# Attention scores from three bf16 parts, FFN tables built during the attention, and value products issued in pairs of sets

## The reference

```python
qkv = layernorm(x) @ Wqkv                       # x: 2 x 1024 x 512; 32 heads of 16, one shared k and v
scores = einsum("bqhd,bkd->bhqk", q, k) * 16**-0.5 + slope[h] * (pos_k - pos_q)   # causal
attn = einsum("bhqk,bkd->bqhd", softmax(scores), v) @ Wo
x = x + layernorm(attn)
W = (code4bit - (zero4bit + 1)) * scale         # Wg, Wu: 512 x 1376, Wd: 1376 x 512, groups of 128 rows
x = x + layernorm((silu(ln(x) @ Wg) * (ln(x) @ Wu)) @ Wd)
```

## Time and profile before

| | |
|---|---|
| median of three runs | 1397.24 us (1396.83 to 1401.67) |
| profiled execution, its own time | 1395.92 us |
| its span, first to last instruction | 1394.1 us |
| mean granted TensorE clock | 0.956 of 2.4 GHz |
| PE, DVE, ACT, POOL busy over the span | 89%, 52%, 41%, 22% |

### The profile page before, as it was taken

One profiled execution on the slowest core, in us unless ns is written; L12 is line 12 of the kernel. 1 busy time (PEld: TensorE's weight loads), 2 busy tenths in 40 slices (PEclk: granted clock), 3 DMA queues, 4 the chain that ended last, 5 costly groups with the idle time before them and its releaser, 6 DMA issues. The chain is left out here.

```text
span 1394.1 us, 16630 instructions
## 1 busy us (share of the span) xinstructions
PE 1239.7 (89%) x6208; PEld 826.8 (59%) x6208; DVE 730.3 (52%) x1353; ACT 571.8 (41%) x1006; POOL 308.0 (22%) x329
## 2 busy tenths in 40 slices
PE   4599999999999999989992389999999999579995
PEld 4567456555554656544541257778778788346664
DVE  4376785786688887723214666342141210365553
ACT  5143455265456565556661344311111111034443
POOL 0121141111110101011124344411121111115554
PEclk9999999899999999999996599999999999889998
DMA  6534223201221012122001422230020010130303
GB/s 194 112 54 113 43 40 106 40 2 39 47 56 25 23 19 40 25 40 40 18 31 51 124 72 62 94 106 0 0 91 1 0 61 1 59 105 1 121 0 120
DMA packets 60942, 75.97 MB, mean 54 GB/s; under 512 B 14738, under 2 KB 37530, under 8 KB 60796
## 3 DMA queue, kind: packets, MB, share of 16 engines
q1 hardware_dynamic: 57252, 64.42, 18.7%
q0 software_dynamic: 2560, 8.39, 1.7%
q10 hardware_dynamic: 1056, 2.16, 0.4%
HBM read 53.46 MB, written 21.59 MB: 54 GB/s over the span
## 5 line engine op out<-in xcount | busy, mean ns | idle before, releaser
L792 DVE TENSOR_REDUCE mx<-bank 128x1 f32<-128x512 f32 (+2 forms) x576 | 367.3, 685 | 138.7 <-PE bank L910 85.1
L734 ACT ACTIVATE PT<-ST 128x512 f32<-128x512 f32 x576 | 313.3, 600 | 210.3 <-PE ST L975 90.0
L907 PE MATMUL bank<-KS,QS 126*128 126x512 f32 (+2 forms) x896 | 253.3, 365 | 18.1 <-DMA QS<-pos_scratch 15.8
L975 PE MATMUL ST<-QS,KS 128*128 128x512 f32 x576 | 240.1, 457 | 5.0 <-DMA QS<-mparts 4.1
L907 PEld LDWEIGHTS bank<-KS,QS 126*128 126x128 f32 x896 | 158.7, 197 | 82.9 <-DVE mx L792 37.7
L975 PEld LDWEIGHTS ST<-QS,KS 128*128 128x128 f32 x576 | 108.3, 195 | 82.6 <-ACT PT L734 64.1
L989 PE MATMUL PO<-PT,V 128*32 128x512 f32 x1152 | 152.2, 604 | 1.6 <-ACT PT L734 1.6
L51 PE MATMUL f_pair<-f_xT,gu 128*128 128x512 f32 (+1 forms) x352 | 142.1, 404 | 0.0
L1495 DVE TENSOR_TENSOR f_h<-f_h,f_pair 128x512 f32<-128x512 f32 (+1 forms) x44 | 30.2, 686 | 210.1 <-ACT f_h L1402 210.1
L53 PE MATMUL f_pair<-f_xT,gu 128*128 128x512 f32 (+1 forms) x352 | 139.8, 397 | 0.0
L52 PE MATMUL f_pair<-f_xT,gu 128*128 128x512 f32 (+1 forms) x352 | 139.4, 396 | 0.0
(11 more groups left out here) (181 smaller groups left out, 1777.6 us busy)
## 6 DMA issues: line engine op xcount, KB each, us to landing
QS<-q_scratch SPq DMA_DIRECT2D x48, 256.0 KB
q_scratch<-QP SPq DMA_DIRECT2D x24, 256.0 KB, 2.3
l_x<-x_dram SPq DMA_DIRECT2D x12, 512.0 KB, 4.2
xres<-_attn_hidden_states_dram POOLq DMA_DIRECT2D x16, 256.0 KB, 3.0
x_dram<-xout POOLq DMA_DIRECT2D x16, 256.0 KB, 2.4
f_xin<-x_dram SPq DMA_DIRECT2D x4, 1024.0 KB, 7.0
f_xsum<-x_dram SPq DMA_DIRECT2D x4, 1024.0 KB, 6.9
x_dram<-f_xsum SPq DMA_DIRECT2D x4, 1024.0 KB, 4.8
```

The lines of the kernel that those rows point to most:

```text
L734: act.activation(PT[:, quad % PT_RING, n % 4, :], ST[:, n % ST_RING, :], ACT.Exp).then_inc(p_done, 1)
L792: v.tensor_reduce(mx[:, i % 2, z, h:h + m], at(u).rearrange("p (m k) -> p m k", m=m), AX.X, ALU.max).then_inc(bank_free_dve, 1)
L907: last = pe.matmul(at(u)[:, j * w:(j + 1) * w], hi(QS[0:ROWS1, slot, h + j, :]), hi(KS[b][0:ROWS1, k0:k0 + w]), start=(j == 0 or not diag) ...
L975: last = pe.matmul(dst, hi(KS[b][0:ROWS2, kb * P:(kb + 1) * P]), hi(QS[0:ROWS2, slot, h:h + 4, :]), start=True, stop=not diag)
```

## The change

1. *Scores.* Queries, keys and maxima are split in three bf16 parts instead of two fp32 ones. The stack has six groups of 16 rows (`Q_PART`, `K_PART`), six rows for positions, written once for each slot, and three for the maxima: 125 or 128 rows. `row_max` and `scores` are bf16 products, in the same number. A query part takes four steps instead of two: ACT, DVE (into `qrest`), ACT (`second_part`), POOL (`query_low`); keys and maxima take ACT, DVE, ACT, DVE. `q_scratch` is written by three transfers for each `q` (was two), a stack is read by six of half the size (was three, and one for positions), maxima by three.
2. *Tables.* Clearing, loading and computing the FFN's tables, unpacking the first two units of codes, and the layer norm and turning of its block 0 (`AFTER`) are steps of the attention's order, let in when the first `row_max` of block `AFTER_AT` = 10 is issued. `ffn` begins with the weight pieces.
3. *Pairs.* The first set of a pair of key blocks waits for all eight exponentials, and the second follows at once. `PT_RING` is 5.

```diff
-POS = slice(3 * HD, 3 * HD + 2)
-ROWS1 = P - 2
+PARTS = 3
+Q_PART = (0, 0, 0, 1, 1, 2)
+K_PART = (0, 1, 2, 0, 1, 0)
+SETS = len(Q_PART)
+POS = slice(SETS * HD, SETS * HD + 2 * PARTS)
+ROWS1 = P - PARTS
-PT_RING = 3
+PT_RING = 5
...
-    took = {"p1": 232, "tile": 232, "pv": 1060, ...
+    took = {"dt": 400, "p1": 218, "tile": 218, "pv": 1060, ...
...
-            deps = [("exp", 4 * q + j) for j in range(4)] + [("v", keys_piece(i))]
+            both = kb % 2 == 0 and kb < BLOCKS[i][1]
+            deps = [("exp", 4 * q + j) for j in range(8 if both else 4)] + [("v", keys_piece(i))]
...
-            out.append((known(*deps), free["pe"] + 1500, ("pv", q)))
+            out.append((known(*deps), -1e9 if kb % 2 else free["pe"] + 1500, ("pv", q)))
...
-            ms = max(ms, 512 // w * 122) + (216 * P // w if diag else 0)
+            ms += 216 * P // w if diag else 0
...
+            if u == maxima_of(AFTER_AT)[0]:
+                sp_issue(("load", AFTER), e)
+                pend["pool"].append((("clear",), e))
+                for k in range(CODE_RING):
+                    sp_issue(("codes", k), e)
...
-                for g, part in enumerate((0, 0, 1)):
+                for g, part in enumerate(Q_PART):
                     sp.dma_start(QS[g * HD:(g + 1) * HD, slot, :, :].rearrange("d (m h) q -> d m (h q)", m=4),
                                  q_scratch[b, qb, part].rearrange("m d h q -> d m (h q)")).then_inc(qs_in[slot], 16)
-                sp.dma_start(QS[POS.stop:POS.stop + 2, slot, :, :], pos_scratch[qb]).then_inc(qs_in[slot], 16)
...
+            def second_part(u):
+                kind, k = u[0][:-1], u[1]
+                freed(act, (kind, *u[1:]))
+                if kind == "q":
+                    m, n = u[2], PIECES[k][2] * P
+                    act.activation(QP[:, 1, m, cols_of(k)], qrest[:, m % 2, 0:n], ACT.Copy).then_inc(q_mid_done, 1)
...
+            def query_low(k, m):
+                pool.wait_ge(q_mid_done, 4 * k + m + 1)
+                n = PIECES[k][2] * P
+                pool.tensor_tensor(QP[:, 2, m, cols_of(k)], qrest[:, m % 2, 0:n], QP[:, 1, m, cols_of(k)], ALU.subtract).then_inc(q_lo_done, 1)
...
-                    last = pe.matmul(at(u)[:, j * w:(j + 1) * w], hi(QS[0:ROWS1, slot, h + j, :]), hi(KS[b][0:ROWS1, k0:k0 + w]),
+                    last = pe.matmul(at(u)[:, j * w:(j + 1) * w], QS[0:ROWS1, slot, h + j, :], KS[b][0:ROWS1, k0:k0 + w],
...
-                last = pe.matmul(dst, hi(KS[b][0:ROWS2, kb * P:(kb + 1) * P]), hi(QS[0:ROWS2, slot, h:h + 4, :]), start=True, stop=not diag)
+                last = pe.matmul(dst, KS[b][0:ROWS2, kb * P:(kb + 1) * P], QS[0:ROWS2, slot, h:h + 4, :], start=True, stop=not diag)
...
-            sp.dma_start(xin[:, :, :], rows(x1_dram, 0)).then_inc(x_in, 16)
-            sp.wait_ge(cleared, 2)
...
-            sp.wait_ge(tables_done, 2)
-            for u in range(len(UNITS)):
-                load_codes(u)
+            sp.dma_start(xin[:, :, :], rows(x1_dram, 1)).then_inc(x_in, 16)
+            for u in range(CODE_RING, len(UNITS)):
+                load_codes(sp, mats, dq, u)
```

More of the change, by code:

```diff
@@ L10 @@
+from collections import namedtuple
 from contextlib import ExitStack
@@ L54, in three_pass, with tile_w, tiles_of, pair_w @@
     return last
+INTER = 1376
+NT = -(-INTER // P)
+PACK, BITS = 8, 4
+GK, GD = 4, 10
+def tile_w(n):
+    return min(P, INTER - n * P)
+TABLE_STEPS = ("index", "onehot", "zeros", "scales", "codes", "dt", "part")
+AFTER_AT = 10
+GROUPS_OF = [GK, GK, GD]
+FIRST_GROUP = [0, GK, 2 * GK]
+G_ROWS = 2 * GK + GD
+S_ROWS = 3 * G_ROWS
+DQ_COL = [0, DC, 2 * DC]
+DQ_COLS = 2 * DC + NT
+PAIRS = -(-NT // 2)
+CODE_RING, WF_RING = 2, 3
+UNITS = [(p, m) for p in range(PAIRS) for m in range(3)]
+def tiles_of(p):
+    return range(2 * p, min(2 * p + 2, NT))
+def pair_w(p):
+    return sum(tile_w(n) for n in tiles_of(p))
+def unit_size(u):
+    p, m = UNITS[u]
+    return (tile_w(2 * p), len(tiles_of(p)) * D) if m == 2 else (P, DC * pair_w(p))
+def unit_loads(u):
+    p, m = UNITS[u]
+    return len(tiles_of(p)) if m == 2 else DC
+def unit_pieces(u):
+    p, m = UNITS[u]
+    if m == 2:
+        return [(i * D, D, [n]) for i, n in enumerate(tiles_of(p))]
+    w = pair_w(p)
+    k = 512 // w
+    k = DC if k >= DC else 2
+    return [(c * w, k * w, list(range(c, c + k))) for c in range(0, DC, k)]
+DQ = [(u, x) for u in range(len(UNITS)) for x in range(len(unit_pieces(u)))]
+def pieces_before(p, m):
+    return sum(u <= 3 * p + m for u, _ in DQ)
+def pieces_during(n):
+    p = n // 2 + 1
+    mine = [j for j, (u, _) in enumerate(DQ) if UNITS[u][0] == p]
+    return mine[0:3] if n % 2 == 0 else mine[3:6]
+EARLY_PIECES = [j for j, (u, _) in enumerate(DQ) if UNITS[u][0] == 0]
+def codes_after(j):
+    u = DQ[j][0]
+    last = j + 1 == len(DQ) or DQ[j + 1][0] != u
+    return u + CODE_RING if last and u + CODE_RING < len(UNITS) else None
 BLOCKS = [(0, qb) for qb in range(QB)] + [(1, qb) for qb in reversed(range(QB))]
@@ L177, in sp_issue @@
             free["sp"] = t + 300
+        elif j[0] == "codes":
+            free["sp"] = t + 2400
+            end["codes", j[1]] = t + 6000
         else:
@@ L313, in commit @@
                     finish_work.append((("wo", i, 1), ("aT", i)))
+            elif kind == "dt":
+                end["bank", j] = f + reads["act"]
+            elif kind == "q2":
+                pend["pool"].append((("q3", *j[1:]), f + 100))
+            elif kind in ("kv2", "mt2"):
+                pend["dve"].append(((kind[:2] + "3", j[1]), f + 100))
+            elif kind == "part":
+                pend["dve"].append((("scales", j[1]), f + 100))
             elif kind == "wo":
@@ L349, in commit @@
             elif kind == "norm":
-                add_piece(j[1], [t + 560 * (x + 1) + reads["dve"] for x in range(3)])
+                add_piece(j[1], [t + 560 * (x + 1) + reads["dve"] for x in range(4)])
+            elif kind == "scales" and j[1] == 0:
+                pend["act"].append((("part", 1), f + 100))
+            elif kind == "index" and j[1] < 3:
+                pend["dve"].append((("index", j[1] + 1), f))
+            elif kind == "index":
+                pend["dve"].append((("onehot",), f))
+            elif kind == "zeros" and j[1] == 0:
+                pend["dve"].append((("zeros", 1), f))
+            elif kind == "zeros":
+                for k in range(CODE_RING):
+                    pend["dve"].append((("codes", k), max(f, end["codes", k])))
+            elif kind == "onehot":
+                end[j] = done
+                for x in range(0, DQ_COLS, 4):
+                    chunk_work.append((("dt", x), j))
             elif kind == "ys":
@@ L626, in _ @@
                     load_x(i)
-            for dst, src in next_loads:
-                sp.dma_start(dst, src, allow_slow_non_contiguous=True).then_inc(next_in, 16)
-            sp.wait_ge(next_in, 16 * len(next_loads))
+                elif kind == "codes":
+                    if i == 0:
+                        full(sp, ("kv", NC - 1))
+                    load_codes(sp, mats, dq, i)
         @block.gpsimd
@@ L939, in fill @@
                         last = pe.transpose(dst[:, t * P:(t + 1) * P], kvf[:, t * P:(t + 1) * P], ident[:, :])
+                elif kind == "dt":
+                    pe.wait_ge(onehot_done, 1)
+                    for k in range(min(4, DQ_COLS - u[1])):
+                        last = pe.matmul(dst[0:S_ROWS, k * P:(k + 1) * P], dq.onehot[:, u[1] + k, :], identb[:, :], start=True, stop=True)
                 elif kind == "mt":
```

562 lines of the change are left out of this document (297 added, 265 removed).

## The result

The changed kernel takes 1317.47 us, median of 4 runs (1316.32 to 1318.83). The kernel before took 1397.75 beside it (1396.83 to 1401.67). The ratio is 0.9421, with a 95% interval of 0.9400 to 0.9442: 80 us less, where 68 were predicted. The profiled execution took 1316.3 us with a span of 1314.5 and a mean clock of 0.965.

The account below looks back on a forecast made before the run. PE was taken to bound the attention, with an idle FFN start besides. PE's need falls 43.7 + 14.5 - 7 = 51 us, 13 given back, leaving 38; with 30 at the FFN start, 68 us, so 1329 us, range 1308 to 1362.

Parts of the forecast that it names:

- the main case: Whole kernel: attention 38 us shorter and FFN start 30 us shorter, 1329 us, own range 1315 to 1343; chance 0.58.
- Score products, sum 43.7: PE in the attention: bf16 tiles and banks save 43.7 us over five kinds of product, ends 34 and 54.
- What PE gets in addition, 7 us: PE in the attention: turned tiles and one-hot products add 2.8 us, fp32r half steps between bf16 scores 4.6.
- The 4.6 for half steps: PE in the attention: about 62 fp32r half steps of q, kv and wo each pay 0.074 us between bf16 scores.
- Pairs, 14.5 us: PE in the attention: 58 more joins of two sets of products with V save 0.25 us each, 14.5 us.
- Given back, 13 us: Attention: 9 us lost to ACT's pace in the last stretch, 3 to the longer query chain; between 0 and 35.
- The rival A, PE starves: Attention: DVE and ACT set the pace, most of the score gain is lost, pairs and FFN start stay; 1352 us, chance 0.22.
- The FFN start, 30 us: FFN block's start: first gate product 16.3 us after the block's first instruction instead of 46.4, 30 us gained.
- The 4.5 us charged for them: FFN start: late codes of unit 2, behind the xin load, delay DVE's weight products and PE's pieces by 4.5 us.
- Nothing behind the gates: FFN after the gates' start: no gain expected, since the order of the work is the same.
- What after would show: Profile signs: scores 0.213 us apart, banks of four about 0.45, attention's last PE product near 703, gate 16 us into block.
- the marks against: Signs of a wrong prediction: banks of four at 0.6 us, PE's bank or ST waits above 35 us, clock below 0.95.

Follow-up runs that it names:

- before_bf16: The kernel before with only its score products in bf16, reading the upper halves of the fp32 elements with a step of two; 1361.89 us, ratio 0.9724.
- no_pairs: The changed kernel with the planner's rule that joins two sets of products with V switched off; 1317.31 us, ratio 0.9415.
- before_pairs: The kernel before with the rule of pairs alone added, score products and tables as they were; 1384.84 us, ratio 0.9888.
- costs_no_pairs: The changed kernel with its attention order planned from durations nearer to the trace, and the rule of pairs off; 1309.26 us, ratio 0.9358.
- codes_first: The changed kernel with the 1 MB load of xin issued behind the codes of units 2 to 5 instead of ahead; 1318.04 us, ratio 0.9419.
- costs_pairs: The changed kernel, pairs kept, with its attention order planned from durations nearer to the trace; 1309.37 us, ratio 0.9347.
- light_pairs: The changed kernel, pairs kept, with maxima over half their keys and exponentials of 256 of 512 columns, values wrong; 1301.47 us, ratio 0.9296.
- light_no_pairs: The changed kernel without the rule of pairs, with maxima over half their keys and exponentials of 256 of 512 columns; 1304.71 us, ratio 0.9307.

## Why the prediction was right, point by point

**The whole.** 1317.5 us was measured, 1329 predicted, in the range of 1308 to 1362 and in the main case's own, 1315 to 1343. The mechanism of each place was right but one, the pairs. The sizes were off in both directions, and that the attention came within 7 us of its forecast is partly luck: the scores gave some 8 more than their sum and the pairs 14 less.

**Score products, sum 43.7: too small.** The prices of single steps hold: a tile or plain bank of 512 saves 0.016 to 0.017 (0.020 foreseen), a bank with mask 0.08 to 0.09 (0.094), 2 x 256 with mask some 0.03, without 0.02 (0.03), 4 x 128 0.184 (0.177). These sum to some 40. (The lower end of the sum is 32 and not 34, with every bank of 2 x 256 at 0.020.) What no row of the sum held is the product behind a set of products with V. PE's timeline of before:

```profile
447.87 1.06 PE L989 MATMUL PO<-PT,V 128*32 128x512 f32 x8
448.86 0.50 PE L975 MATMUL ST<-QS,KS 128*128 128x512 f32 x1
449.20 0.40 PE L907 MATMUL bank<-KS,QS 126*128 126x512 f32 x1
449.44 0.40 PE L975 MATMUL ST<-QS,KS 128*128 128x512 f32 x1
```

of before_bf16, which has the same order:

```profile
430.65 1.06 PE L994 MATMUL PO<-PT,V 128*32 128x512 f32 x8
431.65 0.40 PE L980 MATMUL ST<-QS,KS 128*128 128x512 bf16 x1
431.89 0.39 PE L912 MATMUL bank<-KS,QS 126*128 126x512 bf16 x1
```

and of no_pairs:

```profile
447.82 0.39 PE L1292 MATMUL ST<-QS,KS 128*128 128x512 bf16 x1
448.05 0.38 PE L1220 MATMUL bank<-KS,QS 125*128 125x256 bf16 x2
```

The set takes 1.00 in all three kernels. The tile behind it takes 0.34 in before (448.86 to 449.20), the next 0.24; in before_bf16 it takes 0.24, in no_pairs 0.23. The 104 such products of 512 columns in before have a median of 0.34, in no_pairs it is 0.226. Less the 0.017 that every product saves, and over all 128 sets of before with a score product behind them, that is some 12 us, and the 40 become 52.

A product behind a mask shows a long distance too, 0.32 at 125.88 in the earlier trace rows. That is no second loss. Tiles and masked banks in turn, in before:

```profile
142.70 0.48 PE L975 MATMUL ST<-QS,KS 128*128 128x512 f32 x1
143.02 0.40 PE L907 MATMUL bank<-KS,QS 126*128 126x512 f32 x1
143.26 0.23 PE L910 MATMUL bank<-mask,identb 128*128 128x128 bf16 x1
143.31 0.48 PE L975 MATMUL ST<-QS,KS 128*128 128x512 f32 x1
```

Both together take 0.60, which is the 0.36 of the earlier trace rows and a plain tile's 0.24: the extra of one mask stands here in the tile behind it, and the sum had it in its price for the bank.

**What PE gets in addition, 7 us: too large.** Over all products of PE from 60 us to the last set, start to next start (distances above 1.1 us left out as waits), before has 645 us, no_pairs 598: 48 less, and its last set is 46.7 us earlier. With the scores at some 52, some 4 were added. That fits the turned tiles and one-hot products. The 4.6 for half steps between bf16 scores doesn't show: in before_bf16, with the same order as before, these steps and the products beside them take together what they took, within a us.

**Pairs, 14.5 us: the step that failed.** The price of a join was right (14 us less on PE), and before_pairs gains 12 to 16 us with it. In the changed kernel it is worth 0 (no_pairs), in the better order 0 (costs_no_pairs), and with lighter neighbours 3 to 9. The prediction let the give-back fall on the score part; it fell on the pairs, all of it.

Where it goes shows in codes_first against no_pairs, both with all tiles on record. From 60 us to the last set, each tile and bank is set against the usual distance of its kind. What lies above it is:

- short waits, up to 0.5 us: 13.0 us with pairs, 6.2 without;
- long waits, above 0.5 us: 24 and 14;
- tiles and banks that ran at the 1.2 GHz level: 8.0 (38 of them) and 3.5 (16 of them).

That is 21 us more with pairs. 14 are saved and the other products take 4 less, so the last set is 3.4 later. In costs_pairs and costs_no_pairs, counted over the products whose records are there, the last term is 5.6 and 4.6, and pairs are worth nothing there either, so the clock isn't the reason. Short waits are 8.7 and 2.3 there, long ones 19 and 12.

The short waits go with the pace of DVE and ACT: in light_pairs and light_no_pairs they are 3.4 and 1.6. The long ones stay, 22 and 10. They stand mostly at a block's opening. PE's waits named for `mparts`, `mrest`, `q_scratch`, `A`, `krest`, `aT` and `qrest`, 70 to 660 us, sum to 24 us in after and 17 in no_pairs; the first two of after:

```profile
PE ST L1292 <- DMA QS<-mparts: 7.9, 7, 1.8
PE bank L1220 <- DVE mrest L1082: 4.4, 3, 2.1
```

So the larger part of the loss stands before such chains and stays when DVE and ACT have less to do; the smaller, some 7 us, is short waits behind the two. All this is read from one execution of each kernel, and the medians of the light kernels, 3 apart, don't show a return of 7. Why the chains cost more with pairs is left open.

**Given back, 13 us.** PE's work fell by 48 + 14 = 62 us and the attention ended 45 earlier, so 17 were given back. The size was near, the place wrong: 14 of them are the pairs'. The rival A, PE starves, had the right mechanism for the pairs, and the wrong victim: it had the pairs stay and the scores lost.

**The FFN start, 30 us: right, 32 measured.** The tables' 22.7 us are gone (first piece 0.4 into the block), norm and turns too. The codes of unit 2 were late as said: 8 us into the block. The 4.5 us charged for them were too many; with the codes earlier the gate gained 1.5. No run moves the tables alone. But the FFN start stays at 46.4 us in before_bf16 and 46.3 in before_pairs, so of the three parts of the change only the tables are left to have shortened it.

**Nothing behind the gates: 4 us off.** The order is unchanged there. What follows the first gate takes 594.4 us in before, 595.2 in before_bf16 and 593.1 in before_pairs; with the blocks of after it takes from 590.5 (after) to 594.8 (costs_pairs). So 4 us are within what two executions differ by.

**What after would show.** Held: x16 rows of 1.92, banks of four at 0.44, the gate 14 us into the block, PE's idle time above 25 us. Off: score products 0.218 apart, not 0.213; the attention's last PE product at 696, not 703; the FFN block 13.7 us behind it, not 12; DVE at 73%, where 75 to 80 were foreseen. Of the marks against, one was just met: PE's own waits in front of `bank` and `ST`, 70 to 695 us, sum to 36 us, where 35 was the mark. It pointed at a real loss, that of the pairs.

## What to carry to other kernels

A price from one clean pair of rows holds for its own neighbours only: look at the distances behind each kind of product. Here 104 of 816 products, those behind a set, cost 0.1 us more, and with the rest of their kind that was almost a quarter of what the scores gained. Then test such a group over a whole repetition; the one behind the masks was the known price recorded in another place. Two savings on the same engine don't add once it has slack beside it: pairs gave 12 to 16 us alone, scores 37 (40 to 47 when read in a row), and with both the attention ends 45 earlier. Undo each part in the finished kernel, not only in the old one. And a planner's table of durations ages with the kernel: after such a change new numbers in it gave 8 us, more than the pairs.

## What the runs showed of the hardware that wasn't expected

- A bf16 product of 512 columns that reads its operands with a step of two elements stands 0.229 us from the next, in a row 0.218.
- An fp32r product of 512 columns that follows a set of 32-column products takes 0.34 us to the next instead of 0.233; a bf16 product in the same place 0.226 instead of 0.218 (before and no_pairs; the set takes 1.00 in both).
- DVE's unpacking of 1024 codes takes 0.75 + 0.69 us in after at 717.71, where POOL idles, and 1.52 + 1.64 in codes_first at 716.14, where POOL has products of its own from 715.84 to 718.77. In after the cast at 721.08, beside POOL's product from 720.53, takes 1.64 as well, while the shift at 720.30 takes 0.75. What the two share was not isolated.
- PE ran at half its clock for the first products of the FFN block, behind an idle stretch of 13.7 us: 512 columns 0.42 apart (710.93 to 711.35 in after), the 1.2 GHz level. It did so again from 719.85 to 721.95, behind 5.2 idle us, with the products between at full clock.
